# Ten one-hot tables on one core: the order of the tables, ScalarE's first instructions, and the padding of one table

## The reference

```python
embs = [jnp.dot(x, w) for x, w in zip(xs, ws)]
emb_sum = sum(embs)
q_emb = sum(jnp.dot(xs[i] ** 2, ws[i] ** 2) for i in range(10))
fm_ans = 0.5 * (emb_sum ** 2 - q_emb)
return jnp.concatenate([fm_ans] + embs, axis=-1)
```

## Time and profile before

| | |
|---|---|
| median of 3 runs | 278.85 us (278.64 to 278.89) |
| the profiled execution | 278.5 us |
| its span, first to last instruction | 276.7 us |
| TensorE's mean granted clock | 0.975 of full speed |
| busy: PE, DVE, ACT, POOL | 78%, 81%, 81%, 40% of the span |
| moved by DMA | 113.85 MB, mean 412 GB/s |
| of the chain that ended last | DMA 68%, engines' issue 13%, PE 8%, ACT 8% |

### The profile page before, as it was taken

The page is one execution under the profiler, slowest core; times in us unless marked ns, Lnnn a source line. Parts: engine busy times, 40 slices in busy tenths (PEclk is TensorE's granted clock), DMA queues, the critical chain, the costliest instruction groups (busy, mean ns, idle before and its releaser), DMA issues.

```text
span 276.7 us, 2763 instructions
## 1 busy us (share of the span) xinstructions
PE 215.7 (78%) x892; PEld 153.8 (56%) x892; DVE 225.0 (81%) x150; ACT 225.4 (81%) x280; POOL 110.9 (40%) x78
## 2 busy tenths in 40 slices
PE   0439988799988867969787787778778788689994
PEld 0326756577666545646554555555555565466753
DVE  3677967788799788968978988987987997999885
ACT  0758799999988688979878878877877886899983
POOL 0446665966324109356334134044044041083800
PEclk9975799999999999999999999999999999999999
DMA  7999999999999999999999999999999999999996
GB/s 233 418 394 423 413 438 423 421 422 418 426 430 422 418 420 410 427 421 436 420 429 427 420 431 421 426 421 427 416 429 433 421 420 424 406 416 410 410 395 246
DMA packets 17374, 113.85 MB, mean 412 GB/s; under 512 B 3168, under 2 KB 4448, under 8 KB 11216
## 3 DMA queue, kind: packets, MB, share of 16 engines
q1 hardware_dynamic: 11936, 106.89, 92.7%
q10 hardware_dynamic: 5424, 6.79, 6.8%
HBM read 110.79 MB, written 2.88 MB: 411 GB/s over the span
## 4 chain that ended last, share of the span: by engine, by line
DMA 68%; issue 13%; PE 8%; ACT 8%; DVE 1%; ACTq 1%; SPq 0%
DMA x_ring<-in_x_dram 63%; PE sums L507 7%; ACT is_set L396 6%; DMA whole<-in_w_dram 5%; PE sums L514 1%; ACT whole L386 1%; ACT turned L408 1%; DVE is_one L590 1%; ACTq L373 1%; ACT results L413 0%; DVE total L610 0%; DVE results L633 0%; ACTq L380 0%; ACTq L381 0%; PE sums L552 0%
## 5 line engine op out<-in xcount | busy, mean ns | idle before, releaser
L590 DVE TENSOR_SCALAR_CACHE_REDUCE is_one<-x_ring 128x4096 uint8<-128x4096 f32 (+4 forms) x67 | 221.4, 3320 | 46.5 <-DMA x_ring<-in_x_dram 45.2
L396 ACT ACTIVATE is_set<-x_ring 128x2048 fp32r<-128x2048 uint32 (+2 forms) x112 | 192.2, 1719 | 31.8 <-DMA x_ring<-in_x_dram 31.1
L507 PE MATMUL sums<-is_set,low 128*128 128x512 f32 x398 | 134.7, 419 | 57.3 <-ACT is_set L396 51.7
L507 PE MATMUL sums<-is_set,high 128*128 128x512 f32 x398 | 126.9, 400 | 0.0
L507 PEld LDWEIGHTS sums<-is_set,low 128*128 128x128 f32 x398 | 69.6, 193 | 97.0 <-ACT is_set L396 43.8
L507 PEld LDWEIGHTS sums<-is_set,high 128*128 128x128 f32 x398 | 76.7, 193 | 17.5
L477 POOL CAST high<-whole 128x1024 fp32r<-128x1024 f32 (+5 forms) x31 | 27.0, 872 | 146.6 <-ACT whole L386 146.6
L479 POOL TENSOR_TENSOR low<-whole,high 128x1024 fp32r<-128x1024 f32 (+5 forms) x31 | 60.8, 1961 | 2.5
L396 ACT ACTIVATION_READ_ACCUMULATOR is_set<-x_ring 128x1 f32 (+1 forms) x112 | 21.1, 189 | 0.0
L386 ACT ACTIVATE whole<-whole 128x512 f32<-128x512 f32 (+5 forms) x31 | 16.6, 536 | 4.2 <-DMA whole<-in_w_dram 4.2
L485 POOL TENSOR_TENSOR total<-total,turned 128x1024 f32<-128x1024 f32 x8 | 19.2, 2395 | 0.0
(11 more groups left out here) (29 smaller groups left out, 6.8 us busy)
## 6 DMA issues: line engine op xcount, KB each, us to landing
x_ring<-in_x_dram SPq DMA_DIRECT2D x39, 2048.0 KB, 21.0
x_ring<-in_x_dram SPq DMA_DIRECT2D x19, 512.0 KB, 17.9
x_ring<-in_x_dram SPq DMA_DIRECT2D x6, 1024.0 KB, 21.3
whole<-in_w_dram ACTq DMA_DIRECT2D x19, 256.0 KB, 9.9
x_ring<-in_x_dram SPq DMA_DIRECT2D x3, 1536.0 KB, 21.7
out_dram<-results SPq DMA_DIRECT2D x9, 256.0 KB, 9.3
x_ring<-in_x_dram SPq DMA_DIRECT2D x4, 256.0 KB, 13.8
x_ring<-in_x_dram SPq DMA_DIRECT2D x1, 448.0 KB, 6.3
```

The lines of the kernel that those rows point to most:

```text
L396: nc.scalar.activation(is_set[chunk.k % SETS][0:chunk.rows, 0:length], in_ring(chunk.place, length)[0:chunk.rows].bitcast(U32), ACT.Sign, ...
L507: last = nc.tensor.matmul(sums[:, summing(n, half), :], w, x[0:chunk.rows, at:at + HALF], start=first, stop=False, skip_group_check=True)
L590: nc.vector.tensor_scalar(is_one[c % 2][0:rows, 0:length], in_ring(at, length)[0:rows], 1.0, None, ALU.is_equal, ALU.add, accum_out=one_co ...
```

## The change

Three things change. Table 1 (49 tiles) moves from the seventh place of `ORDER` to the first, ahead of the six small tables 8, 9, 5, 4, 7 and 3. Its first group is loaded and counted by 2 tiles at a time in place of 4, which makes 74 transfers and 68 counts (of 72 and 66). Table 9's tile is padded to 128 rows, in DRAM too, so that no instruction on x is narrower than 128 partitions. On ACT a square of one column, from a constant to a tile that nothing reads, stands ahead of everything, and the squares of the first two groups stand behind the first and the second `count_set` in place of ahead of them.

```diff
-TAIL = [-(-(v - P * (tiles - 1)) // 16) * 16 for v, tiles in zip(VOCABS, TILES)]
+TAIL = [-(-(v - P * (tiles - 1)) // 16) * 16 if tiles > 1 else P for v, tiles in zip(VOCABS, TILES)]
...
 ORDER = [
+    (1, [FULL] * 6 + [[1]]),
     (8, [[1, 1]]),
     (9, [[1]]),
...
     (3, [[2, 2, 2], [2, 1, 1]]),
-    (1, [FULL] * 6 + [[1]]),
     (6, [[2, 2, 2, 1, 1]]),
...
-            most = 2 if group.table == LAST else LOAD
+            most = 2 if group.table == LAST or not group.g else LOAD
...
-                sp.dma_start(in_ring(load.at, load.length)[0:load.rows],
+                sp.dma_start(in_ring(load.at, load.length),
...
             act.wait_ge(constants, 8)
-            for group in GROUPS[:AHEAD - 1]:
-                square(group)
+
+            nc.scalar.activation(unused[:, :], ones[:, :], ACT.Square)
             for group in GROUPS:
                 for c, chunk in enumerate(group.chunks):
                     count_set(chunk)
+                    if chunk.k < AHEAD - 1:
+                        square(GROUPS[chunk.k])
```

More of the change, by code:

```diff
@@ L69, in __init__ @@
         self.tail = tile + n == TILES[table]
-        self.rows = TAIL[table] if TILES[table] == 1 else P
         self.group = self.count = None
 class Load:
-    def __init__(self, i, table, tile, n, first, width, rows, at):
-        self.i, self.table, self.tile, self.n, self.rows, self.at = i, table, tile, n, rows, at
+    def __init__(self, i, table, tile, n, first, width, at):
+        self.i, self.table, self.tile, self.n, self.at = i, table, tile, n, at
         self.first, self.width, self.length = first, width, n * width
@@ L89, in __init__ @@
         self.c, self.loads, self.chunks = c, loads, chunks
-        self.at, self.length, self.rows = loads[0].at, sum(load.length for load in loads), loads[0].rows
+        self.at, self.length = loads[0].at, sum(load.length for load in loads)
         for chunk in chunks:
@@ L162, in plan_counts @@
         for tile, n in parts:
-            own.append(Load(len(loads) + len(own), one.table, tile, n, one.first, one.width, one.rows, at))
+            own.append(Load(len(loads) + len(own), one.table, tile, n, one.first, one.width, at))
             at += own[-1].length
@@ L337, in _ @@
                 base = zeros = 0
-                for t in G_ORDER:
+                for t in range(NT):
                     end, rows = TILES[t] - 1, TAIL[t]
@@ L396, in count_set @@
                 nc.scalar.activation(
-                    is_set[chunk.k % SETS][0:chunk.rows, 0:length],
-                    in_ring(chunk.place, length)[0:chunk.rows].bitcast(U32), ACT.Sign,
-                    accum_out=set_counts[0:chunk.rows, chunk.k:chunk.k + 1]).then_inc(set_counted, 1)
+                    is_set[chunk.k % SETS][:, 0:length], in_ring(chunk.place, length).bitcast(U32),
+                    ACT.Sign, accum_out=set_counts[:, chunk.k:chunk.k + 1]).then_inc(set_counted, 1)
             def copy_sums(n):
@@ L502, in multiply @@
                     for part in (low, high):
-                        w = part[group.pair][0:chunk.rows, chunk.at + t, :]
+                        w = part[group.pair][:, chunk.at + t, :]
                         first = chunk.k == BEGIN[n] and t == 0 and part is low
@@ L507, in multiply @@
                             last = nc.tensor.matmul(sums[:, summing(n, half), :], w,
-                                                    x[0:chunk.rows, at:at + HALF], start=first,
-                                                    stop=False, skip_group_check=True)
+                                                    x[:, at:at + HALF], start=first, stop=False,
+                                                    skip_group_check=True)
                 last.then_inc(x_multiplied, 1)
@@ L628, in _ @@
             part = final.length // 2
-            count_ones(final.at, part, final.rows, NCOUNTS - 1)
+            count_ones(final.at, part, NCOUNTS - 1)
             for half, blocks in enumerate(halves):
```

16 lines of the change are left out of this document (7 added, 9 removed).

## The result

The changed kernel takes 279.36 us (median of 10 runs, 279.11 to 280.44), the kernel before 278.81 us beside it. The ratio is 1.0025, with a 95% interval from 1.0014 to 1.0035: slower by 0.25%, a little over what can be told from no change. The prediction was 278.3 us: the time lies inside its range (277.6 to 279.5), but on the other side of the kernel before.

A forecast was written before the change was run, and what follows sets the result against it. The prediction took DMA transfers to bound the kernel. Its terms, -0.55 + 0.15 - 0.24 + 0.1 + 0 = -0.54 us, gave 278.3 us for the median, with a range of 277.6 to 279.5.

The forecast's parts named there:

- What bounds the kernel: Whole run: the middle is transfer work at 420 to 424 GB/s; engines' time doesn't count while transfers wait in the queue.
- Table 9 with 128 rows: Start, 5.5 to 7.75 us: 16 more rows cost +0.15 us, the slow stretch of the 112-row load goes, -0.55 us.
- nothing at the start is won: Rival, first 8 us: the slow stretch returns whatever is loaded; padding and smaller transfers remain, +0.25 us, 279.1; chance 20%.
- First packets and 2-tile loads: Table 1 first: early packets of 8192 bytes in place of 4096 win 0.24 us; transfers of 2 tiles cost +0.1 us.
- What the small packets pay back: Small tables' packets moved to 65 to 105 us cost the same work there: counted 0, bounds -0.5 and +0.3.
- The waits of SP: Loads issued only when ACT is done with the tiles in their place: spare 0.7 us of queue, so counted 0.
- Spare: 3.7 - 3.0 - 1.5 + 1.5 = 0.7 us: Queue's spare work, less 2 tiles of lead, less new ACT work, plus ACT being 13.2 us behind and not 14.7.
- the queue runs dry behind table 6: Rival, about 110 to 120 us: ACT late when table 0's third load is due, DMA idles; 279.6 to 281.6, chance 17%.
- the tightest lead: Behind the small tables: the tightest wait stands 12 tiles ahead in place of 14, 3.0 us less.

The follow-up runs named there:

- 21 places: Changed kernel with one is_one buffer in place of two and the ring at 21 places, not 20: 278.11 us, ratio 0.9982; control with 20 places 279.29 us.
- table 6 ahead: Changed kernel with table 6 moved ahead of the small tables, right behind table 1: 282.38 us, ratio 1.0137.

## Why the prediction was wrong

**What bounds the kernel:** right, as far as the runs go. The gains and losses that were traced to a stretch are gains and losses in GB/s, and ScalarE's earlier start alone moved nothing that could be told. The end moved with x, 1 to 1: from the start of DVE's last count of 4 tiles it is 37.1 us to the end in the changed kernel (240.2 to 277.3) and 37.2 before (239.5 to 276.7).

**Table 9 with 128 rows:** right, and its size nearly so. The sum had -0.55 + 0.15 = -0.40 us, the padding alone measured -0.5. The rival "nothing at the start is won" fell with it. The reason that the prediction gives, the shape of the transfer, held against the placing in DRAM too.

**First packets and 2-tile loads:** -0.24 + 0.1. The changed kernel moves 57 GB/s up to 2.5 us against 41, so 40 KB or 0.1 us more, where I had 0.24. I did not separate the rest.

**What the small packets pay back:** counted at 0, and so it came out, within 0.1 us. By 9.75 us the changed kernel is 0.41 MB ahead (1.0 us), and from 20 to 60 us it wins another 0.16 MB (424 against 420 GB/s); from 60 to 110 us, where it has the small tables, it moves 414 GB/s and gives 50 x (1 - 414/424) = 1.2 us back. The new order without its dips (278.11, 21 places) is as fast as the old order with the same padding (278.15): no gain from table 1's being first can be told.

**The waits of SP:** this step failed. It was "Spare: 3.7 - 3.0 - 1.5 + 1.5 = 0.7 us ... So I count 0 for this". The term measured +1.2 us: that is what the changed kernel's dips come to, and what the 21st place of the ring gives back (279.29 to 278.11). The mechanism and the place are those of the rival "the queue runs dry behind table 6", which had 17%. Its cause of the further lag was a wait for weights of 2 to 4 us, and its times were 279.6 to 281.6; the new wait was 1.33 us, and the time lies at its shallow end. And only the smaller dip belongs to the load that it named, table 0's third.

How late ScalarE would be at table 6's first load I had right: 13.2 + 1.5 = 14.7 us, and 14.7 it was, though by other parts than I listed (0.93 us of waiting for PE ahead of table 1's copy and 1.33 us for table 6's weights were new, 0.6 us of the wait for table 4's weights went). That the total came out to 0.1 us is luck in part. What was wrong for this load is, by the numbers, what a load costs when the queue is at its end; no run varied it alone. I gave "about 1 us" to the time ahead of the first packet, besides 6.0 us for the 4 tiles, so 7.0 us; the two loads took 7.9 and 8.3. The first load of the kernel could have told: it was issued at 0.8 us, and only 25 packets had moved by 2.5 us. That 0.9 to 1.3 us more turns a spare of 0.7 into a lack of 0.2 to 0.6, and the dip of this load is 0.44 us. The other, larger dip I had not priced at all: I looked at the tightest lead alone, 12 tiles, and not at the load ahead of it with its 13, where ScalarE was later still, 15 us behind, with the wait for table 6's weights just ahead of its chunks.

A spare of 0.7 us at the end of a sum of several terms, when one of them alone turned out 0.9 to 1.3 us off, is not a zero. It should have stood in the sum as an even chance of something between 0 and 2 us.

## What to carry to other kernels

In a kernel bound by transfers through a ring, count for every load how many tiles it is ahead of the one that it waits for, in the engine that frees them last, and set this against how late that engine is at this point; here they met right behind the small tables. A load that doesn't fit in front of the ring's end shortens the lead without a trace in the program's order. Work that makes an engine late cost nothing where the ring was still empty, which is where the old order had it. And a large transfer to fewer than 128 partitions is worth filling up: here 64 KB of zeros more took 0.5 us off.

## What the runs showed of the hardware

In these kernels the rate falls while a large transfer to fewer than 128 partitions is in progress. Table 9's 448 KB in 112 rows cost about 0.5 us at the start (296 GB/s for 2.25 us) and 1.3 us in mid-run, beside packets of 4 KB in both places, so their size doesn't explain the difference; it stays open. Two halves of 64 rows made 241 GB/s of the 2.25 us. The rows don't tell whether this transfer's own packets are slow or those beside it. The Trainium skill, "DMA: Bandwidth & Descriptors", section on the descriptor swizzle, gives each of the 16 engines one port in a transfer over 128 partitions; its page "SBUF — State Buffer", section on the DMA port swizzle, says that partitions 0 to 63 reach only 8 of the 16 ports. That a 64-row half is the slowest of the shapes agrees with it; the traces don't show ports. Narrow weight transfers (16 to 112 rows of 256 bytes) occur in every kernel here. Beside those of 84 to 91.5 us in the kernel before, 422 to 434 GB/s were moved, so no such loss shows there.

The times of the kernels whose queue runs dry scatter more: 279.11 to 280.44 for the changed one and 280.89 to 283.52 with table 6 ahead, against 277.90 to 278.35 with 21 places. A likely reason, not tested, is that whether a load comes a little early or late at an empty queue differs from one execution to the next.
